# GNN megakernel on one core: source rows gathered once per edge tile into a ring, and copied from there to the steps

## The reference, cut to what matters

```
def gatv2_layer(x, src, dst, Wl, bl, Wr, br, att, bias):
    xl = x @ Wl + bl
    xr = x @ Wr + br
    xj = xl[src]                                   # gather
    e = leaky_relu(xj + xr[dst], 0.2)
    logits = e @ att
    ex = exp(logits - segment_max(logits, dst)[dst])
    alpha = ex / (segment_sum(ex, dst)[dst] + EPS)
    return segment_sum(alpha[:, None] * xj, dst) + bias
```

## Time and profile before

| | us |
|---|---|
| median of three executions | 12959.7 |
| span of the profiled execution | 12943.7 |
| mean granted TensorE clock | 0.775 |
| POOL busy | 9352.2 (72%) |
| PE busy | 10725.3 (83%) |
| DVE busy | 7913.5 (61%) |
| ACT busy | 5610.6 (43%) |

### The profile page before, as it was taken

How to read it: one execution, slowest core, us unless ns; L and a number is a source line. 1 busy time by engine, 2 the same in 40 slices (tenths; PEclk the granted TensorE clock), 3 DMA queues, 4 the chain that set the end, 5 groups by cost and what they waited for, 6 DMA issues and landing times.

```text
span 12943.7 us, 281524 instructions
## 1 busy us (share of the span) xinstructions
PE 10725.3 (83%) x62317; PEld 8649.8 (67%) x62317; DVE 7913.5 (61%) x29130; ACT 5610.6 (43%) x14105; POOL 9352.2 (72%) x8593
## 2 busy tenths in 40 slices
PE   5788887788888878888888886999999878888886
PEld 4666666666666666666666665777777656666664
DVE  7666666666666655555555555333333568888887
ACT  1555555455555553333333335344444543333334
POOL 3777777577777758888888885777777447777775
PEclk7999999899999966666666667555555688889887
DMA  3222222422222224444444445222222222222222
GB/s 96 56 55 55 55 55 55 132 65 56 56 56 56 55 42 39 39 39 39 39 39 39 38 39 131 57 56 56 56 56 56 58 65 62 62 61 63 61 61 61
DMA packets 809108, 749.26 MB, mean 58 GB/s; under 512 B 264686, under 2 KB 691175, under 8 KB 808255
## 3 DMA queue, kind: packets, MB, share of 16 engines
q0 software_dynamic: 453440, 550.05, 24.5%
q1 hardware_dynamic: 354814, 191.38, 5.7%
HBM read 548.62 MB, written 192.13 MB: 57 GB/s over the span
## 4 chain that ended last, share of the span: by engine, by line
PE 52%; issue 9%; DVE 8%; DMA 6%; POOL 2%; ACT 2%; DVEq 2%; SPq 0%; POOLq 0%; ACTq 0%
PE bank L721 13%; PE bank L705 7%; PE bank L708 6%; DMA scatter_s<-dst_side 6%; PE bank L706 5%; PE bank L1181 4%; PE bank L1187 3%; PE bank L730 3%; PE bank L690 2%; PE bank L1196 2%; POOL scatter_s L1148 2%; DVE agg L929 1%; DVE dst_side L1274 1%; DVE lrelu L884 1%; PE bank L1190 1%
## 5 line engine op out<-in xcount | busy, mean ns | idle before, releaser
L1148 POOL DMA_INDIRECT scatter_s<-dst_side x1664 | 2566.9, 1543 | 555.4 <-DMA scatter_s<-dst_side 240.1
L808 ACT ACTIVATE oh_e<-bank,weight,minus_w 128x128 f32<-128x128 f32 x4992 | 1876.2, 456 | 1465.3 <-PE bank L730 1385.3
L920 DVE SCALAR_TENSOR_TENSOR agg<-agg,rescale,bank 128x130 f32 x4992 | 1680.8, 337 | 1211.0 <-PE bank L721 958.6
L706 PE MATMUL bank<-rows,ident 128*128 128x128 f32 x9984 | 2108.6, 296 | 0.0
L672 POOL DMA_INDIRECT rows<-gather_c,edge_sb x1664 | 1631.9, 981 | 599.6 <-issue 382.3
L672 POOL DMA_INDIRECT rows<-gather_b,edge_sb x1664 | 1605.9, 965 | 608.5 <-issue 314.8
L672 POOL DMA_INDIRECT rows<-gather_a,edge_sb x1664 | 1622.8, 975 | 555.4 <-issue 315.5
L672 POOL DMA_INDIRECT rows<-gather_s,edge_sb x1664 | 1570.3, 944 | 571.3 <-issue 378.7
L721 PE MATMUL bank<-rows,oh_e 128*128 128x130 f32 x9984 | 1873.4, 343 | 54.1 <-DVE agg L920 37.1
L721 PEld LDWEIGHTS bank<-rows,oh_e 128*128 128x128 f32 x9984 | 1601.6, 242 | 268.5 <-issue 230.4
L706 PEld LDWEIGHTS bank<-rows,ident 128*128 128x128 f32 x9984 | 1695.0, 213 | 0.0
(11 more groups left out here) (345 smaller groups left out, 19310.3 us busy)
## 6 DMA issues: line engine op xcount, KB each, us to landing
rows<-gather_a,edge_sb POOLq DMA_INDIRECT x1664
rows<-gather_b,edge_sb POOLq DMA_INDIRECT x1664
scatter_s<-dst_side POOLq DMA_INDIRECT x1664, 3.4
rows<-gather_s,edge_sb POOLq DMA_INDIRECT x1664
rows<-gather_c,edge_sb POOLq DMA_INDIRECT x1664
rows<-scatter_s SPq DMA_DIRECT2D x56, 455.0 KB, 6.1
scatter_s<-zeros SPq DMA_DIRECT2D x64, 390.0 KB, 5.7
edge_sb<-edge_tab SPq DMA_DIRECT2D x520, 40.0 KB
```

Of the source, the lines that this page charges most:

```text
L706: e.matmul(o, ident[:, :], rows[:, it.slot(), g, 0:P], start=False, stop=True).then_inc(L.side.sem, 1)
L808: e.activation(oh_e[:, g % 8, :], bank[7][:, (g % CH) * P:(g % CH + 1) * P], ACT.Relu, bias=weight[:, it.slot(2, 2), g:g + 1], scale=minus ...
L920: e.scalar_tensor_tensor(old, old, rescale[:, it.slot(2, 2), g:g + 1], sum_bank(g)[:, (g % 2) * AW:(g % 2) * AW + L.aw], ALU.mult, ALU.add ...
L1148: e.indirect_dma_start(scatter_s[k], bass.IndirectOffsetOnAxis(ap=S_.target[:, it.slot(1), g:g + 1], axis=0), S_.summed[:, g % 8, :], None ...
```

## The change

Three passes (E0, E1, E2) gather by tile and no longer by step. The preparation makes two more things: `tile_tab`, which has for every 16 tiles their source indices by column, and for each chunk of 4 tiles a number of steps; and, in `row_tab1`, for every group the place (0 to 15) in a ring at which each step's tile lies, and, for each chunk of steps, the counts of landed gathers to wait for. POOL gathers NGT = 98 times 16 tiles into the ring (it takes the memory of `xw` and `row_sb`), and waits, once per chunk of tiles, for the landing of the chunk two back and until `side` has been done for all steps of the tiles that lie there. SP waits for a chunk's tiles and copies them, row block by row block, with 16 DMAs per group from the ring to `rows`. Behind the last four copies of a group it issues the table loads of the next group, and the columns of two turns on.

```
-            turns(e, NG, 0, turn)        # sp_edges, for E0, E1, E2
+        def sp_staged(e, L):
+            def tables(it, lag):
+                u, i = it.slot(lag), it.number() - lag
+                w.hold_ge(L.acc.at(it, G - 1, lag=U + lag))
+                w.hold_ge(L.tab.at(it, lag=U + lag))
+                ... the four table loads ...
+            def columns(it, lag):
+                for c in (NCH - 2, NCH - 1):
+                    w.hold_ge(L.landed(it, c, lag=2 * U + lag))
+                w.hold_ge(L.cols.at(it, lag=U + lag))
+                e.dma_start(tile_sb[:, it.slot(lag, 2 * U), :], tile_tab[...]).then_inc(L.cols.sem(it, lag), 16)
+            def turn(it):
+                u = it.slot()
+                w.hold_ge(L.tab.at(it))
+                row = L.row_ring[0:1, u, R1:RS].bitcast(I32)
+                place = step_values(e, mybir.EngineType.SP, row[:, 0:G], 0, G - 1)
+                even = step_values(e, mybir.EngineType.SP, row[:, G:G + NCH], 0, FETCHED)
+                odd = step_values(e, mybir.EngineType.SP, row[:, G + NCH:], 0, FETCHED)
+                (sem0, base0), (sem1, base1) = L.fetched
+                for c in range(NCH):
+                    w.hold_ge(L.block.at(it, c, lag=U))
+                    w.hold_ge((sem0, (even[c] & 0x7fff) + base0))
+                    w.hold_ge((sem1, (odd[c] & 0x7fff) + base1))
+                    for g in range(c * CH, (c + 1) * CH):
+                        e.dma_start(rows[:, u, g, 0:L.width], ring[:, bass.ds(place[g], 1), :].rearrange("p o f -> p (o f)")
+                                    ).then_inc(L.gat[c].sem(it), 16)
+                    if c == NCH - 1:
+                        if it.runs(-1, NG):
+                            tables(it, -1)
+                        if it.runs(-2, NG):
+                            columns(it, -2)
+                if it.j is None:
+                    for table, z0, z1 in L.zeroing[it.n::PEEL]:
+                        e.dma_start(table[z0 * P:z1 * P, :]..., zeros[...]).then_inc(L.zeroed, 16)
+            tables(Turn(0), 0)
+            columns(Turn(0), 0)
+            columns(Turn(0), -1)
+            turns(e, NG, 0, turn, ahead=2, per=2 * U)
+        def pool_staged(e, L):
+            def turn(it):
+                u, first = it.slot(0, 2 * U), it.j is None and it.n == 0
+                w.hold_ge(L.cols.at(it))
+                if not first:
+                    done = step_values(e, mybir.EngineType.Pool, tile_sb[0:1, u, G:TC], 1, S + NB)
+                for c in range(NCH):
+                    w.hold_ge(L.landed(it, c - 2) if c >= 2 else L.landed(it, c + 2, lag=1))
+                    if not first:
+                        w.hold_ge((L.side.sem, (done[c] & 0x7fff) + L.side.base))
+                    for g in range(c * CH, (c + 1) * CH):
+                        e.indirect_dma_start(ring[:, g, :], None, L.src_rows,
+                                             bass.IndirectOffsetOnAxis(ap=tile_sb[:, u, g:g + 1], axis=0)
+                                             ).then_inc(L.fetched[c % 2][0], 16)
+            turns(e, NGT, 0, turn, per=2 * U)
@@ pe_edges, side
                 w.wait_ge(L.onehot_t.at(it, c))
+                if L.vector or L.staged:
+                    w.wait_ge(L.gat[c].at(it))
                 if L.vector:
-                    w.wait_ge(L.gat[c].at(it))
@@ dve_prep_rows: the places in the ring and the counts
+            first, tile_f, tile_i = more(0, 1), more(1), more(2).bitcast(I32)
+            ... ten small operations on 104 rows of 1, 4 or 16 values ...
@@ act_dense0, sp_prep, pe_prep: for each of 13 tables of 128 tiles
+                e.copy(tile_src_f(c), tile_src(c))          # ACT
+                e.transpose(bank[c % 2][:, 3 * P:4 * P], tile_src_f(c), ident[:, :])   # PE
+                e.copy(tile_out(c)[:, :, 0:G], bank[c % 2][:, 3 * P:4 * P]...)         # ACT, and one for the counts
+                e.dma_start(tile_tab[c * GC:(c + 1) * GC, :, :]..., tile_out(c))       # SP, and one to load src
```

More of the change, by code:

```diff
@@ L35, with __init__ @@
 class Turn:
-    def __init__(self, n, j=None):
-        self.n, self.j = n, j
+    def __init__(self, n, j=None, per=U):
+        self.n, self.j, self.per = n, j, per
     def runs(self, lag, of):
@@ L48, in number @@
     def number(self):
-        return self.n if self.j is None else self.j * U + self.n
+        return self.n if self.j is None else self.j * self.per + self.n
 class Signal:
@@ L64, in at @@
             return (self.sem, value) if it.n >= lag else None
-        return self.sem, it.j * (self.each * U) + value
+        return self.sem, it.j * (self.each * it.per) + value
 class Landing:
@@ L84, in at @@
             return (self.sem(it, lag), value) if it.n >= lag else None
-        return self.sem(it, lag), it.j * self.gain + value
+        return self.sem(it, lag), it.j * (self.gain * it.per // len(self.sems)) + value
 class Counts:
@@ L145, in hold_ge, with turns @@
                 self.eng.sem_inc(self.anchor, 1)
-def turns(eng, n, depth, turn, ahead=0):
+def turns(eng, n, depth, turn, ahead=0, per=U):
     assert ahead <= U
-    end = n - U if ahead else n
+    end = (n - U if ahead else n) // per * per
     for i in range(PEEL):
         turn(Turn(i))
-    with eng.Fori(PEEL // U, end // U) as j:
-        for u in range(U):
-            turn(Turn(u, j))
+    with eng.Fori(PEEL // per, end // per) as j:
+        for u in range(per):
+            turn(Turn(u, j, per))
     for i in range(end, n + depth):
@@ L320, in build @@
         prevlast, change = grp(3), grp(4)
-        row1 = spare(2 * P, R1)[0:NG, :]
+        row1 = spare(2 * P, RS)[0:NG, :]
+        more = lambda k, n=G: spare(8 * P + k * G, n)[0:NG, :]
         row8 = spare(3 * P, R8)[0:NG, :]
@@ L371, in sp_prep @@
                 sp_dense0(e, D, "D", c)
+            save_columns(SC - 1)
+            for c in range(SC, SC + -SC % U):
+                e.sem_inc(tile_src_in.sem(c), 16)
+            for c in range(SC, SC + SC % 2):
+                e.sem_inc(tile_saved.sem(c), 16)
+                e.sem_inc(step_saved.sem(c), 16)
             w.wait_ge(edges_made.at(SC - 1))
@@ L595, in __init__ @@
                 self.SW = 3 * P + 2 if heads > 1 else 2 * P + 2
-                self.rw = R8 if heads > 1 else R1
+                self.staged = staged is not None
+                self.rw = R8 if heads > 1 else RS if self.staged else R1
+                self.row_ring = row_sb8 if heads > 1 else row_sb1
+                if self.staged:
+                    self.fetched = staged
+                    self.cols = counts.landing("tile_columns_in", U, 1, NG)
+                    self.gat = [counts.landing(name, 2, CH, NG) for name in ("residual_saved", "table_saved", "nodes_in", "step_rows_saved")]
+                else:
+                    self.gat = [counts.landing(f"rows_in_chunk{c}_slot", U, CH, NG) for c in range(NCH)]
                 self.row_tab = row_tab8 if heads > 1 else row_tab1
@@ L602, in __init__ @@
                 self.tab = counts.landing("tables_in_slot", U, 3 + heads, NG)
-                self.gat = [counts.landing(f"rows_in_chunk{c}_slot", U, CH, NG) for c in range(NCH)]
                 self.dist, self.side, self.edist = four("distances"), each("side_sums"), four("edge_distances")
@@ L625, in __init__, with landed @@
                 self.zeroing, self.zeroed = [], None
+            def landed(self, it, c, lag=0):
+                if it.j is None and it.n < lag:
+                    return None
+                sem, base = self.fetched[c % 2]
+                return sem, (it.number() - lag) * (8 * NCH * CH) + 16 * CH * (c // 2 + 1) + base
             def w_last(self, it, lag, c):
```

140 lines of the change are left out of this document (115 added, 25 removed).

## The result

The changed kernel takes **14,057.6 us** (median of 4 runs, 14,048.2 to 14,064.7) against 12,962.1 beside it: ratio **1.0847**, 95% interval 1.0832 to 1.0863. It is 1,096 us slower; I had said 12,920, with 13,200 as the upper end.

What follows compares the result with a forecast made beforehand. POOL was taken to bound E0 and E1, PE to bound E2. E0 -64, E1 +2, E2 +5, openings +15 and preparation +4 gave -38 us: 12,906 on the profiled span, 12,920 as median, range 12,780 to 13,200.

Steps and rivals of the forecast that it cites:

- E0: First of the three passes, bound by POOL: 19.85 us a group instead of 20.47, so -64 us.
- E2: Third pass, bound by PE at the 1.2 GHz level: 0 to +29 us, +5 taken; forecast wrong if over 30.
- the loop: PE's side frees the ring, POOL gathers, SP loads and copies, PE goes on: 20.4 us from group to group.
- POOL's part: In each pass 1568 gathers replace 1664: 123 us less POOL time, 19.3 us a group; its register load taken as 0.
- SP's part: SP's turn of loads, holds, 16 copies, tables and columns: 16.5 us a group, no bound by itself.
- The loop closes in two of four groups: Over one group the loop rules half of the groups at 20.4 us, POOL's 19.3 the others: mean 19.85.
- Tables: PE's wait in chunk 2 for the next group's tables, issued behind chunk 3's copies: nothing taken, bound +1 us a group.
- E1's zeros: SP's zero writes in E1 stand between tables and next copies: +57 us, so E1 +2 against E0's -64.
- the copies queue behind the writes: Rival in E1: chunk 0's copies of eight groups wait for zero writes to land, +45 us, 12,960; chance 0.08.
- POOL's pace: Rival: shorter loads and landing put the loop under 19.3 us, POOL's pace reached in full, 12,790; chance 0.20.
- SP too slow: Rival: SP's copies at 0.73 us pass today's group time; at 0.75 us each the total is 13,190; chance 0.22.
- PE's clock: Rival: longer waits lower PE's clock from 0.94 to 0.75 in E0 and E1, +310 us, 13,220; chance 0.06.

Runs made afterwards that it cites:

- both mends: The changed kernel with register loads aligned to 16 bytes and the next group's tables issued behind the third chunk's copies: 13,015.4 us, ratio 1.0056.
- the best version: The kernel with both mends, but E2 gathers by step again and ACT, not SP, issues E1's zero writes: 12,957.2 us, ratio 1.0015.

## Why the prediction was wrong

The step that failed is the loop: its sum was 20.4 us, with three register loads at 3.3, and it was taken to hold in two of four groups and to cost nothing through PE's wait for tables. The groups took 24.0 us, and aligning the loads and issuing the tables earlier gave 1,042 of the 1,096 us back.

- **POOL's part: right in size, with one cover missed.** 1568 gathers, 0.978 + 0.305 us, as said. Its register load I took at 0 "because the sequencer comes to it while gathers are queued"; with both mends, load and waits together are 0.9 us a group, three quarters of what the saved gathers are worth.
- **SP's part and the loop: the step that failed.** Prediction's terms against this trace: `side` 0.7, 0.7; gathers and landing 6.5, 6.5; holds and four copies 2.5, 3.2; tables 3.2, 3.6; register loads 3.3, **5.3**; second holds and copies 2.05, 2.6; landing 2.2, 2.3. Sum 20.4 forecast, **24.2** with the measured terms, and a group takes 24.0. That the two agree is in part chance: the loads are 5.3 only in three slots of four (1.8 in the fourth), so the mean of the sum is 23.3, and `side` takes nearly twice its 0.7 after a long wait, as the window at 0.52 shows. The loads are 2.0 of the 3.8: three loads at 1.10 were wrong both ways, 0.07 us a value (1.75 for all 24) where aligned, 0.215 (5.2) where not. I costed a load by its count of instructions and never compared the ring's strides, 1696 bytes before and 356 after, although both stand in the code. 1.25 is copies and holds: a copy issues every 0.645 us, 0.51 and 0.13 of register work, not 0.55; three holds take 0.45 to 0.6 us, not 0.3 or 0.4.
- **"The loop closes in two of four groups": wrong too.** With the measured terms my halving, (24.2 + 20.6 for SP's own turn)/2, gives 22.4 at most, not 24.0; and with aligned loads even a loop of 20.65 in every group is short of the 22.2 that the groups take. So some 1.6 us a group or more is in no term. Group times in E0 swing between 17 and 32 us with no spare tile in the ring and no table ahead; that such swings do not average out is my reading, which no run isolates, and PE at the lower clock after its waits is another, as little isolated.
- **Tables: taken at 0, +1 us a group as bound.** They stood in the loop, as the sum says, and cost 443 to 465 us, 1.4 to 1.5 a group. I had put them in the loop and then nothing for PE's wait; the wait at L844 was 2.2 us a group. That PE's slack did not cover it because it lay in the same loop is my reading.
- **E1's zeros: right in size, and the cause as said for SP's writes.** E1 grew by 441 us and E0 by 366, 75 more; the forecast was +2 against -64, 66 more. The rival in which the copies queue behind the writes did not come: in each of the eight groups of the changed kernel the first copy behind the writes is issued 4.2 to 8.8 us after them, and its DMA events end 1.8 to 2.3 us after its issue, as elsewhere. With 4.2 us between them, this says little on what a queue would do with copies close behind. **Preparation: right**, +4 us.
- **E2: wrong by the same step.** PE stays at the 1.2 GHz level and is busy 83% instead of 94%; it waits for the copies. E2 moved by 302 us, where the forecast called itself wrong from 30.
- **The rivals.** POOL's pace is not reached even with both mends (20.35 against 19.3). SP too slow comes nearest to what happened, but not by its price: it was to decide at 0.73 us a copy, and the copy is at 0.645. By its slope, 7 issues of the loop, which no run tested, 0.095 us too much a copy is 0.67 of the 3.8 us. PE's clock did fall, 0.94 to 0.83, and PE's busy time grew by 1.7 us a group while it waited for more than that. It reads as an effect, since both mends, which touch no matmul, bring it back to 0.90; and E2 lost 302 us with its clock at 0.50 before and after. (That rival's total should read 13,230 by its own terms.)
- **The two engines I left out.** PE's and DVE's loads at three times their price are worth 163 us on their own. They were in no term.

## What to carry to other kernels

When a table's row changes length, look at the address of everything that an engine's queue reads from it into registers: three words of padding were worth 577 us here. A stage that joins two engines through a third closes a loop, and everything in that third queue's turn is in it; take loads and tables out of the turn before counting what the first engine saves. Count what the new bookkeeping costs the engine that is relieved: of the 123 us a pass that POOL was to save, 25 came out in E0 of the best version, and 12 to 35 in three executions with both mends; E1 and E2 gained nothing.

## What was not expected of the hardware

- A register load from SBUF costs by the value, 0.07 us (16 in 1.15, 4 in 0.30), when it starts at a multiple of 16 bytes, and 0.215 us (3.45, 0.87) in each slot where it does not. The Trainium skill (Runtime: NRT & Kernel Launch, section "Instruction fetch mechanics") gives some 200 ns a register for loads from HBM; these loads are from SBUF, so no run here tests that figure.
- Copies of 128 x 512 bytes within SBUF issue every 0.645 us back to back. The last one of a chunk lands 2.0 us after its issue (median of the 104 chunks of E0 whose DMA events are all in the trace; 1.84 to 3.5 for nine in ten).
- An issue is dearer beside others: a write of zeros 0.45 us in lots of two or three and 0.82 in lots of eight or nine, a copy by SP 0.51 us alone and 0.82 beside ACT's writes.
- Two kinds of chips: on three of the six used, SP's queue pauses for up to 1.4 us in ordinary instructions (seen in the traces of all three), the kernel before takes 16 to 17% longer, and a kernel with a busy SP suffers more (ratio 1.0488 where the others show 1.0056).
